# Queries stored in DRAM already expanded to 64 rows and loaded in two transfers, and GpSimd's square taken before the last step of the split

## The reference

```python
x = x + 0.5 * ffn0(layernorm(x))       # r * (square(relu(xk @ Wk.T)) @ Wv.T), r = sigmoid(xr @ Wr.T)
x = x + causal_attention(layernorm(x)) # 16 heads of 8, causal, softmax clipped
x = x + 0.5 * ffn0(layernorm(x))
x = x + 0.5 * moe(layernorm(x))        # 8 experts, the best 2
x = x + focus_attention(layernorm(x))  # 3 iterations: qcur = qcur + out, scores from normalised heads
x = x + 0.5 * moe(layernorm(x))
```

## Time and profile before

| | us |
|---|---|
| median of 3 runs | 1375.23 (1371.81 to 1378.19) |
| profiled execution | 1369.53 |
| its span | 1367.8 |
| PE busy | 1217.5 (89%) |
| DVE busy | 920.0 (67%) |
| ACT busy | 842.2 (62%) |
| POOL busy | 533.9 (39%) |
| mean granted TensorE clock | 0.966 of full speed |
| DMA | 125.77 MB in 113582 packets |

### The profile page before, as it was taken

How to read it: one execution, slowest core, us unless ns; L and a number is a source line. 1 busy time by engine, 2 the same in 40 slices (tenths; PEclk the granted TensorE clock), 3 DMA queues, 4 the chain that set the end, 5 groups by cost and what they waited for, 6 DMA issues and landing times. The chain is left out here.

```text
span 1367.8 us, 36731 instructions
## 1 busy us (share of the span) xinstructions
PE 1217.5 (89%) x12275; PEld 781.6 (57%) x12275; DVE 920.0 (67%) x2874; ACT 842.2 (62%) x1549; POOL 533.9 (39%) x817
## 2 busy tenths in 40 slices
PE   4689899898759999999889988999899997999998
PEld 3456566566537777777544433444344443767876
DVE  3578888887746874677677745666766665677444
ACT  3467777776433344443677877899787885333543
POOL 6366766766430040401344433344333331032344
PEclk9799999999959999999999999999999999999999
DMA  6323323324204022111545544445434441001332
GB/s 162 93 66 93 97 58 104 92 64 106 53 7 139 3 76 84 55 32 52 142 120 155 151 126 113 144 137 141 126 111 126 122 119 39 1 28 41 102 115 85
DMA packets 113582, 125.77 MB, mean 92 GB/s; under 512 B 14988, under 2 KB 90020, under 8 KB 113450
## 3 DMA queue, kind: packets, MB, share of 16 engines
q1 hardware_dynamic: 110378, 117.82, 30.6%
q0 software_dynamic: 3072, 6.30, 1.5%
HBM read 79.89 MB, written 44.05 MB: 91 GB/s over the span
## 5 line engine op out<-in xcount | busy, mean ns | idle before, releaser
L1469 ACT ACTIVATE e_buf<-ps_q 128x1024 f32<-128x1024 f32 x192 | 196.9, 1026 | 58.0 <-PE ps_q L2194 57.7
L2207 PE MATMUL ps_o<-e_buf,v_st 128*32 128x256 f32 x3072 | 210.7, 393 | 5.1 <-POOL v_st L1081 4.2
L1469 ACT ACTIVATE e_buf<-ps_k 128x1024 f32<-128x1024 f32 x192 | 197.0, 1026 | 7.5 <-PE ps_k L2194 7.4
L2054 PEld LDWEIGHTS ps_o<-w,e_buf 128*128 128x128 f32 x1280 | 152.2, 193 | 13.1 <-issue 12.0
L2054 PE MATMUL ps_o<-w,e_buf 128*128 128x128 f32 x1280 | 158.4, 277 | 0.0
L2622 DVE TENSOR_REDUCE mx<-ps_q 128x10 f32<-128x640 f32 x128 | 104.9, 820 | 45.0 <-PE ps_q L1752 44.1
L1290 ACT ACTIVATE e_buf<-ps_k 128x768 f32<-128x768 f32 x128 | 103.0, 805 | 46.2 <-PE ps_k L1764 45.3
L2207 PEld LDWEIGHTS ps_o<-e_buf,v_st 128*32 128x32 f32 x3072 | 81.5, 110 | 76.6 <-issue 40.3
L940 POOL TENSOR_SCALAR_AFFINE_SELECT e_buf<-e_buf 128x512 f32<-128x512 f32 x128 | 85.6, 669 | 89.8 <-ACT e_buf L1290 86.9
L1385 ACT ACTIVATE e_buf<-ps_q,b_t 128x512 f32<-128x512 f32 x80 | 54.6, 685 | 90.5 <-PE ps_q L2046 86.7
L1385 ACT ACTIVATE e_buf<-ps_k,b_t 128x512 f32<-128x512 f32 x80 | 54.0, 685 | 71.0 <-PE ps_k L2046 67.6
(11 more groups left out here) (392 smaller groups left out, 2746.5 us busy)
## 6 DMA issues: line engine op xcount, KB each, us to landing
k_st<-scr_x SPq DMA_DIRECT2D x128, 256.0 KB
q_st<-scr_q SPq DMA_DIRECT2D x256, 96.0 KB
scr_q<-parts SPq DMA_DIRECT2D x64, 192.0 KB, 2.0
scr_x<-parts SPq DMA_DIRECT2D x48, 192.0 KB, 2.0
q_st<-scr_q SPq DMA_DIRECT2D x128, 64.0 KB
slots_in<-heads_out SPq DMA_DIRECT2D x3, 1536.0 KB
slots_out<-heads_out SPq DMA_DIRECT2D x18, 256.0 KB
heads_out<-slots_in SPq DMA_DIRECT2D x15, 256.0 KB
```

Of the source, the lines that this page charges most:

```text
L1469: act.activation(e_buf[g % 2][:, hp * 2 % HG:hp * 2 % HG + 2, :], (ps_q, ps_k)[hp % 2][:, :, :], ACT.Exp).then_inc(sem("fast_exp"), 1)
L2054: last = mm(ps_o[:, e % 2, t * P:(t + 1) * P], h_sb[e % 2][:, f, t * P:(t + 1) * P], w2[:, e * NF + f, :], start=f == 0, stop=f == NF - 1)
L2207: last = mm(ps_o[at:at + VW, p, low:low + T], v_st[p][:, kt, h, :], e_buf[g % 2][:, j, kt * T:(kt + 1) * T], start=g == 0 and kt == 0, sto ...
```

## The change

Two edits.

The first: queries are stored as keys are. `scr_y` holds, for each `p`, eight planes of 128 x 256. `query_blocks` writes them with three DMAs (3, 3 and 2 copies of a part), in the place of the one store of 384 runs; `query_halves` loads them with two DMAs of 64 rows in the place of six. Counts of semaphores are changed to fit. The general path, which this input does not take, still reads `scr_q`.

The second: in POOL's causal round `causal_last_parts(n + 1)` moves from before `mix_square` to behind `causal_keep(n, 3)`.

```diff
             def query_halves(p, landed):
 
                 for u in range(2):
-                    for j, n in enumerate(PARTS):
-                        low = 64 * u + 3 * HD * j
-                        sp.dma_start(q_st[p][low:low + n * HD, 0:HP, :].rearrange("r h t -> r (h t)"),
-                                     bass.AP(scr_q.tensor, p * 3 * PLANE + u * HP * T, [[H * T, n * HD], [1, HP * T]]))\
-                            .then_inc(landed, 16)
+                    rows_u = scr_y[p].rearrange("(r u n) -> u r n", u=2, n=HP * T)[u]
+                    sp.dma_start(q_st[p][64 * u:64 * u + ROWS_T, 0:HP, :].rearrange("r h t -> r (h t)"), rows_u)\
+                        .then_inc(landed, 16)
+
+            def query_blocks(p, which, done):
+
+                for j, n in enumerate(PARTS):
+                    sp.dma_start(scr_y[p].rearrange("(i c t) -> c i t", c=C, t=T)[:, j:8:3, :],
+                                 parts[:, which, j, :].unsqueeze(1).broadcast_to([P, n, T])).then_inc(done, 16)
@@ fast_operands
-                sp.dma_start(bass.AP(scr_q.tensor, p * 3 * PLANE, [[T, C], [PLANE, 3], [1, T]]),
-                             parts[:, p, :, :]).then_inc(sem("fast_parts_out"), 16)
-                sp.wait_ge(sem("fast_parts_out"), f * 16 + 16 + 32)
+                query_blocks(p, p, sem("fast_parts_out"))
+                sp.wait_ge(sem("fast_parts_out"), f * 48 + 48 + 96)
@@ causal_operands
-                sp.dma_start(bass.AP(scr_q.tensor, p * 3 * PLANE, [[T, C], [PLANE, 3], [1, T]]),
-                             parts[:, 0, :, :]).then_inc(sem("parts_out"), 16)
+                query_blocks(p, 0, sem("parts_out"))
...
-                sp.wait_ge(sem("parts_out"), f * 16 + 32)
+                sp.wait_ge(sem("parts_out"), f * 48 + 96)
@@ POOL, causal_round
                 causal_keep(n, 2)
-                if parts_next:
-                    causal_last_parts(n + 1)
                 if first:
                     mix_square(mix1(n + 3))
                     mix_gate(mix1(n + 3))
                 causal_keep(n, 3)
+                if parts_next:
+                    causal_last_parts(n + 1)
@@ PE, row_scores and pair_scores
-                    pe.wait_ge(sem(f"fast_operands_in_{p}"), half * 128 + 128)
+                    pe.wait_ge(sem(f"fast_operands_in_{p}"), half * 64 + 64)
```

More of the change, by code:

```diff
@@ L327, in macaron_kernel @@
         scr_k = nc.dram_tensor("scr_k", (B, 3 * PLANE), BF16, kind="Internal").ap()
+        scr_y = nc.dram_tensor("scr_y", (2, 8 * PLANE), BF16, kind="Internal").ap()
         scr_x = nc.dram_tensor("scr_x", (B, 8 * PLANE), BF16, kind="Internal").ap()
@@ L618, in operands @@
                     hold()
-                sp.wait_ge(sem("parts_out"), (n + B) * 16 + 32)
+                sp.wait_ge(sem("parts_out"), n * 16 + B * 48 + 64)
                 hold()
@@ L697, in general_focus @@
                             max_rows(n, p)
-            sp.sem_inc(sem("fast_parts_out"), 32)
+            sp.sem_inc(sem("fast_parts_out"), 96)
             sp.sem_inc(sem("K_out"), 48 * GB)
-            sp.sem_inc(sem("parts_out"), 16)
+            sp.sem_inc(sem("parts_out"), 48)
             sp.sem_inc(sem("k_parts_out"), 48)
@@ L1274, in causal_parts @@
                 act.wait_ge(sem("qk32"), f * 2 + 2)
-                act.wait_ge(sem("parts_out"), f * 16 + 16)
+                act.wait_ge(sem("parts_out"), f * 48 + 48)
                 act.wait_ge(sem("k_parts_out"), f * 48 + 48)
@@ L3137, in front_parts @@
                 dve.wait_ge(sem("query_nt"), f + 1)
-                dve.wait_ge(sem("fast_parts_out"), f * 16 + 16)
+                dve.wait_ge(sem("fast_parts_out"), f * 48 + 48)
                 hold()
```

## The result

The changed kernel took 1400.99 us (median of 6 runs, 1395.32 to 1407.04), the kernel before 1372.38 us (6 runs, 1366.87 to 1378.19) on the same chip: ratio 1.0211, 95% interval 1.0186 to 1.0236, so 28.6 us slower where 7.8 were forecast. The profiled execution has a span of 1400.3 us, 32.5 more than before.

The account below looks back on a forecast made before the run. Focus steps were taken as bound by a query store-and-load chain paid once every two steps, causal rounds by POOL's queue. 12 legs x 0.65 = +7.8 us, causal 0, on 1375.23 gave 1383 us; 8-in-10 range 1367 to 1392.

Parts of the forecast that it names:

- Causal rounds: Causal stage: query stores start 2.4 us later, no stall expected on average; 0 us, up to +6 in the range.
- The cover of some 2.4 us: Causal rounds: slack before PE's first use of the loaded keys, some 2.4 us, used up by the later stores.
- warm queue: Causal rounds: unsized saving taken off the keys' arrival at 216.6, against PE's first use at 216.65.
- The forecast's own sign of being wrong: Causal rounds: PE waiting for `q_st` would show the forecast wrong; no size given.
- rival C: Causal rounds: late operands exceed the cover, 12 rounds wait 0.5 us each, +6 us, 1389 in all; chance 0.14.
- Rival A: Causal rounds: the earlier square shortens 11 rounds by 1.15 to 1.36 us, -13 to -15, 1369 in all; chance 0.15.
- Store leg: Focus step, first store to loads: three stores of 512 KB instead of one of 192, +0.9 us, bounds +0.75 and +0.95.
- Load leg: Focus step, queries' load issue to data: two issues instead of six, -0.25 us, ends 0 and -0.6.
- The far end of 0.6: Focus step, queries' load: largest gain, 0.6 us, if it started as early as the old or 16 engines replaced 12.
- Second and third iteration: Focus stage: the second pays 7 legs of 0.65 us; the third has 1.8 us of slack and pays nothing.
- First iteration: Focus stage: 5 legs of 0.65 us on the chain through its 8 waits.
- Which does not make it cheaper: First focus iteration: the query store also queues behind the keys' stores; no size was given.

Follow-up runs that it names:

- order alone: Kernel before with only POOL's new causal order, stores and loads as they were: 1455.99 us, ratio 1.0066 (chip where the kernel before takes 1447.56).
- expansion alone: Changed kernel with POOL's old causal order put back: 1462.64 us, ratio 1.0115 to the kernel before (1447.56 us on that chip).

## Why the prediction was wrong

The direction was right (slower, the likeliest of the three), the size was not: 1401 against 1383, outside the range that ended at 1392. Where the causal rounds lost it shows in the ten middle rounds of four traces (medians, us; a landing is the last completion in the loads' semaphore; "order alone" and "expansion alone" are the second and the first experiment):

| | before | order alone | expansion alone | changed |
|---|---|---|---|---|
| first exponential to first store | 7.6 | 9.9 | 7.6 | 9.9 |
| first store to landing of the keys | 9.8 | 9.7 | 10.3 | 10.4 |
| of this, from the queries' first load | 7.3 | 7.2 | 6.8 | 6.8 |
| of this, from the keys' first load | 4.7 | 4.6 | 5.5 | 5.5 |
| landing to first scores | 2.3 | 0.2 | 1.8 | 0.2 |

- **Causal rounds, the step that failed.** The forecast said: "With 3.6 us for the data and some 0.8 until PE sees it ... The cover of some 2.4 us is used up; I expect no stall on average". The delay and the unchanged 5.1 us to the keys' issue were right. First scores start 0.2 us behind the landing where nothing else holds them, so the cover was 2.1 us, and the delay of 2.3 takes all of it. What the expansion adds, 0.6 us from first store to landing, then comes on top; alone it takes 0.6 of the cover and costs nothing. Together that is about the 0.7 us by which rounds 5 to 12 grew (20.67 to 21.35). The term that was mis-sized is the keys' load: 4.4 us from issue to PE in the forecast, 4.9 in the kernel before, 5.7 in the changed one. The forecast credited the loop with the 1.15 us that two loads save in issuing and left the data at 3.6. But the keys' data follows half a megabyte of queries through the same engines, so an earlier issue mostly means a longer wait there: the 1.15 us bought 0.5 (7.3 and 6.8 in the table). The saving that the forecast expected of a "warm queue" is shown by no run. I also put the miss at "0.5 us a round" at most; but here, where the loop is closed, the late operand is paid in full every round, 0.7 us in the steady ones, 0.8 to 2.6 in rounds 2 to 5 and 1.5 to 2 in the last two. The forecast's own sign of being wrong, PE waiting for its loads in the causal rounds, has come true (13.6 us in 12 times). This is rival C, whose price was 6 us where it was 14.
- **Rival A** was rightly held unlikely. PE's wait of 16.6 us for the square went, and the steady rounds were no shorter, even where nothing was late (early stores in both stages).
- **Store leg.** +0.9 us forecast, +0.9 measured (2.11 and 3.01). Behind it are two causes: 0.4 to 0.5 us for three transfers, 0.4 for volume.
- **Load leg.** -0.25 forecast, as measured: from issue to the last data 3.95 us before and 3.7 after (medians of the second and third iteration). That the shares of the earlier trace rows show 12 engines was read too much into them: the 24-row loads' quarters have 0.45 to 0.60, under the 0.75 of 12 engines. The far end of 0.6 was out of reach, since the first packet comes 1.3 us behind the issue, against 0.9 before.
- **Second and third iteration.** +4.5 forecast and +2.9 measured; 0 and 0.2, over the last 14 steps of each.
- **First iteration, the other term that was too small.** 5 legs of 0.65 were 3.3 us, measured 12.9. "Which does not make it cheaper" stood where a price belonged. From first store to loads its 16 steps are 24.1 us longer than before in sum, 1.5 us each, against 0.9 in the second iteration. The excess sits in five steps that are 2.0 to 3.3 us longer: three met an instruction packet in the changed kernel (two of them met none before), two stand directly behind late keys' stores. Moving the stores about 2 us forward gave 8.8 us of this iteration back; moving the keys' stores out of the way gave 1.4. How a packet delays a store is shown by the DMA records: in the step above, in that of the store at 760.71 (packet until 764.65, the store's last packets from 764.63) and in the kernel before (packet until 814.44, last packets from 814.43) the rest of the store begins when the packet ends. That it waits on the very engine that fetches is inferred from this. The fetch itself could not be taken away, so how much of the 12.9 us it costs stays open.
- **Sum.** 14.3 (causal) + 0.9 (to the focus stage) + 12.9 + 1.9 (first and second iteration, from first scores to first scores) = 30.0 us at the start of the third iteration, of 32.5 us in the profiled execution. The other 2.5 lie behind it and were not followed up.

## What to carry to other kernels

Before moving a producer later, close the loop: add up producer to store, store to load, load to consumer and consumer to the next producer, with durations taken from the very place, and compare with the period; what is beyond it is paid in every round. When transfers follow each other into the same engines, take the time from the first issue of the group to the last landing: here the second went out 1.3 us sooner behind the first, and the last landing came 0.5 sooner. And before expanding data in DRAM to save descriptors on the load, price the store: more transfers and more volume stood in front of the load that was to gain.

## What the runs showed that I had not expected

- Issuing a store earlier did not make the loads start earlier in the second iteration, where a keys' load issued just before it fills the engines: with expanded stores 3.3 us behind the last part in place of 3.1, with small ones 2.4 in place of 2.2. In a causal round, with no load in front, the same move brought them from 3.7 to 1.9 us behind the last part.
- A DMA whose outermost dimension is 2 ran on two engines (share 0.12 to 0.13) and made the kernel 20% slower, though it had fewer transfers and not one byte more.
- Splitting one store of 192 KB in three on a critical leg cost 0.4 to 0.5 us in a typical step and 13 us of 1370 in all.
- A single 16 KB instruction packet in a step went with a landing of 3.8 us (median) in place of 2.2, and of 3.1 in place of 2.1 in the kernel before.
